# Four routing steps move to the odd iteration, and a normalisation moves behind the routing's places

## The reference

```python
h = tokens + pos_embed                                   # embedding
h = h + local_attn(layernorm(h), w_qkv, w_proj, b_proj)  # windowed attention
flat = layernorm(h).reshape(-1, 192)
probs = softmax(flat @ router_w.T)                       # 8 experts
top_w, top_i = top_k(probs, 2)
top_w = top_w / top_w.sum(-1)
for e in range(8):
    w_e = sum(top_w * (top_i == e), -1)
    out += w_e * (gelu(flat @ w1[e] + b1[e]) @ w2[e] + b2[e])
h = h + out
```

## Time and profile before

| | |
|---|---|
| median of 3 runs | 1567.22 us (1561.56 to 1568.72) |
| the profiled execution | 1561.32 us, of which the span 1559.5 us |
| TensorE matmul (PE) busy | 1429.6 us, 92% of the span |
| VectorE (DVE) busy | 1105.2 us, 71% |
| GpSimd (POOL) busy | 900.7 us, 58% |
| ScalarE (ACT) busy | 665.5 us, 43% |
| mean granted clock of TensorE | 0.973 of full |

### The profile page before, as it was taken

How to read it: one execution, slowest core, us unless ns; L and a number is a source line. 1 busy time by engine, 2 the same in 40 slices (tenths; PEclk the granted TensorE clock), 3 DMA queues, 4 the chain that set the end, 5 groups by cost and what they waited for, 6 DMA issues and landing times.

```text
span 1559.5 us, 51122 instructions
## 1 busy us (share of the span) xinstructions
PE 1429.6 (92%) x17688; PEld 1190.2 (76%) x17689; DVE 1105.2 (71%) x2824; ACT 665.5 (43%) x1150; POOL 900.7 (58%) x899
## 2 busy tenths in 40 slices
PE   4999998999999999999777789999999999999995
PEld 4788887888888888888555567777777777777774
DVE  2578887886877888788654776666666666666663
ACT  2455455454545455454435333333333333333331
POOL 4236566555656556565334875666666666666655
PEclk9999999998999999999878999999999999999998
DMA  5665665656565565655334375555554455555552
GB/s 173 182 183 151 196 169 151 187 162 174 162 198 159 154 192 158 186 165 159 76 64 78 72 150 81 76 75 74 73 75 72 74 78 74 75 73 74 75 72 31
DMA packets 305662, 189.18 MB, mean 121 GB/s; under 512 B 201977, under 2 KB 291397, under 8 KB 304477
## 3 DMA queue, kind: packets, MB, share of 16 engines
q1 hardware_dynamic: 241706, 118.06, 30.6%
q0 software_dynamic: 41680, 41.84, 17.8%
q10 hardware_dynamic: 22115, 27.08, 5.5%
HBM read 89.79 MB, written 65.29 MB: 99 GB/s over the span
## 4 chain that ended last, share of the span: by engine, by line
PE 53%; DVE 18%; POOL 9%; issue 9%; ACT 4%; ACTq 4%; DMA 2%; SPq 1%; DVEq 0%; POOLq 0%
PE qk L1086 7%; PE qk L1087 7%; PE qk L1088 7%; PE scores L1073 7%; PE near L1073 6%; ACTq L599 3%; POOL sorted_scratch L498 3%; PE far L1073 3%; PE token_bank L1073 3%; PE mixed L1073 3%; PE qk L1182 3%; DVE qk L978 3%; POOL payload L508 2%; DVE st L758 2%; PE near L1119 2%
## 5 line engine op out<-in xcount | busy, mean ns | idle before, releaser
L498 POOL DMA_INDIRECT sorted_scratch<-payload,place x212 | 223.6, 1055 | 57.8 <-issue 57.2
L1119 PE MATMUL near<-we,both_patches 128*120 128x192 f32 x1272 | 224.4, 334 | 19.2 <-DMA both_patches<-in_xt 11.6
L572 ACT ACTIVATE stage<-near,bias 128x384 f32<-128x384 f32 x118 | 68.5, 581 | 383.6 <-PE near L1073 368.0
L1119 PEld LDWEIGHTS near<-we,both_patches 128*120 128x120 f32 x1272 | 208.6, 186 | 29.7 <-issue 27.7
L483 POOL DMA_INDIRECT out<-both_patches,token x111 | 205.9, 1855 | 36.2 <-issue 36.0
L483 POOL DMA_INDIRECT out<-v_side,token x108 | 198.1, 1834 | 38.6 <-issue 37.9
L1086 PE MATMUL qk<-w_hi,stage 128*128 x666 | 165.5, 248 | 5.1 <-DVE v_side L911 5.1
L1086 PE MATMUL qk<-w_hi,both_patches 128*128 x648 | 160.2, 247 | 8.0 <-issue 4.1
L1088 PE MATMUL qk<-w_hi,we 128*128 x666 | 165.4, 248 | 0.0
L1087 PE MATMUL qk<-w_lo,stage 128*128 x666 | 165.4, 248 | 0.0
L1088 PE MATMUL qk<-w_hi,both_patches 128*128 x648 | 160.1, 247 | 0.0
(11 more groups left out here) (259 smaller groups left out, 3711.5 us busy)
## 6 DMA issues: line engine op xcount, KB each, us to landing
both_patches<-in_xt SPq DMA_DIRECT2D x53, 720.0 KB
v_diag<-v_scratch SPq DMA_DIRECT2D x159, 89.2 KB
v_scratch<-v_side SPq DMA_DIRECT2D x53, 191.2 KB, 3.7
tabs<-tab_scratch SPq DMA_DIRECT2D x53, 180.0 KB
out<-h ACTq DMA_DIRECT2D x52, 180.0 KB
stage<-in_w ACTq DMA_DIRECT2D x8, 1152.0 KB
k_diag<-qk SPq DMA_DIRECT2D x436, 15.8 KB
stage<-in_w ACTq DMA_DIRECT2D x8, 576.0 KB
```

Source lines behind the costliest of these rows:

```text
L498: pool.indirect_dma_start(out=sorted_dram, out_offset=bass.IndirectOffsetOnAxis(ap=at, axis=0), in_=payload[0:rows, 2 * (block % RING) + n ...
L572: act.activation(act_out[:, m, :], bank_of(u, m), ACT.Gelu, bias=bias[k % 2][:, m:m + 1], scale=1.0 / WS).then_inc(s["gelu_done"], 1)
L1119: ins = pe.matmul(near[0:ROWS, n * D:n * D + D], patches[f % 2][:, x, n * ROWS:n * ROWS + ROWS], we[:, x, :], start=(x == 0), stop=(x == K ...
```

## The change

The 26 steps are cut at two more points (`PART_AT`). The first four steps of the former part 1 (L802 to L805: the best expert masked, the second largest logit, where it is, times the ranks) become part 1 and run in the odd iteration right behind part 0; `choose(1)` and `marks` become part 2 and stay in the even one. The former part 3 is cut behind the places (part 4) and before the wait for the shares (part 5). In even iterations with routing due, `normalise` of the embedded block moves behind parts 3 and 4, ahead of part 5; in all others it moves behind the split of the expert weights (and behind the list of batches in iteration 51, and the splits of the attention weights in iteration 0). The step number that ScalarE's `second_share` waits for stays 7 in its group.

```diff
-PART_AT = (0, 5, 11, COUNTS_READ, STEPS)
+SECOND_AT = 7
+PART_AT = (0, 5, 9, 11, COUNTS_READ, 18, STEPS)
...
-                    act.wait_ge(s["step"], STEPS * grp + PART_AT[1] + 2)
+                    act.wait_ge(s["step"], STEPS * grp + SECOND_AT)
...
                     then(dve.tensor_tensor(tmp[:], tmp[:], ranks, ALU.mult))
+                if part == 2:
                     choose(1)
...
-                if part == 2:
+                if part == 3:
...
-                if part == 3:
+                if part == 4:
                     for j in range(CHOSEN):
...
-
+                if part == 5:
 
                     dve.wait_ge(s["weighed"], grp + 1)
...
                 if due:
-                    route_steps(grp, 1)
+                    route_steps(grp, 2)
...
-                if runs(t, 0):
-                    normalise(h1[f % H_RING], mv1, rs1, xn1, "1", f + 1)
                 if t == 0:
...
                 if due:
-                    route_steps(grp, 2)
                     route_steps(grp, 3)
+                    route_steps(grp, 4)
+                if runs(t, 0) and due:
+                    normalise(h1[f % H_RING], mv1, rs1, xn1, "1", f + 1)
+                if due:
+                    route_steps(grp, 5)
...
                     ins.then_inc(s["split_lo"], 1)
+                if runs(t, 0) and not due:
+                    normalise(h1[f % H_RING], mv1, rs1, xn1, "1", f + 1)
                 if due_0:
                     route_steps(grp_0, 0)
+                    route_steps(grp_0, 1)
```

## The result

The changed kernel takes 1586.68 us (median of 4 runs, 1583.38 to 1602.62), the one before 1567.26 in the same comparison: 1.0144 times as long (95% interval 1.0094 to 1.0194; it isn't the quotient of the two medians, 1.0124). The forecast was 1562.6, with a range of 1546 to 1577. The profiled execution after took 1583.38 us, 22 more than that of before; 19.8 of them lie in iterations 8 to 51. Lines of the file after stand 1 to 7 further down (L978 is L985, L812 is L814, L691 is L692).

A forecast was written before the change was run, and what follows sets the result against it. A ring through VectorE, ScalarE and TensorE was taken to bound the kernel. Pairs -12.7, +1.3 and +7.4, old low clocks -7.4, new ones +9.5, edges -2.7: together -4.6, from 1567.22 to 1562.6 us, range 1546 to 1577.

The forecast's parts named there:

- the count's wait: Even iteration: VectorE waits 0.8 us for TensorE's count before the places, where it waited 1.11 for GpSimd's `rs`.
- The odd cost: Odd iteration: four added steps and a meeting with GpSimd's L526 make L978 later by 0.9 to 1.4 us, taken 1.16.
- TensorE's 1.40: Odd iteration: TensorE's 1.40 us stand before its transposes, from a late exponential, would go.
- step 5 of the even iteration: VectorE's eight remaining steps end earlier, so L978 starts 2.6 us earlier, net 2.4, in ten even iterations.
- Three falls: Three of six even iterations where ScalarE issues an expert's weights fall to a low clock, 3.15 us each: +9.5.
- three old ones: Low clocks of odd iterations 19, 31 and 37 go: -7.4 us.
- The rival "slower": Clock falls in every weight iteration (8, 14, 20, 32, 38, 44), 5.2 us each: +17.1, 1584.3 us; chance 0.15.
- The full gain: Rival: odd iteration's added steps slip past L526, costing 0.89, and no new clock falls: -20.0, 1547.2 us; chance 0.25.
- Nothing: Rival: the `rs` wait and the moved steps are slack on VectorE, so no change: 1567.2 us; chance 0.12.
- the ring: Closed chain bounding iterations 8 to 51, 28.8 us a pair: VectorE's attention output, ScalarE's exponential, TensorE's logits, back to VectorE.
- The start: Iteration 0: the normalisation and its wait no longer stand ahead of L951, for which TensorE waits: 1.5 us less.

The follow-up runs named there:

- N: Against the kernel before, only the normalisation moved, in even and odd iterations; the four steps stay in the even one: 1548.35 us, ratio 0.9924.
- the extra steps: Four extra steps of the same shapes, on a scratch tile, added to N in the odd iteration: 1572.44 us, ratio 1.0126.

## Why the prediction was wrong, point by point

**Right: the parts that were read off one engine.** In iteration 24, L939 starts 0.80 after the exponential (forecast 308.43 - 307.62 = 0.81, before 2.47); the count's wait ends at 2.98 (3.18) and is 0.63 (0.8); L820 ends at 4.69 (4.68). L809 lasts 0.19. The odd cost from the logits to the low half is 2.52 - 1.53 = 0.99 in the mean (1.16, range 0.9 to 1.4). The trace agrees with the rule of the Trainium skill that the forecast weighed (SBUF — State Buffer, Who interferes with whom): L806 and L489 pay 0.79 and 0.91. TensorE's 1.40 ahead of the transposes is gone from iteration 23; in the odd iterations 14 stands of 0.2 to 2.6 became five of 0.3 to 0.7, and in the six weight iterations it stands 1.24 to 2.28.

**Wrong: step 5 of the even iteration, and with it the sum.** It said that L978 starts 2.6 earlier, net 2.4, in ten iterations, 0.9 in five, 0.1 in seven: 29.2 us, 1.33 a pair. Measured from the exponential to the attention output it is 11.50 - 11.01 = 0.49 against the first profile and 0.17 against the second. Over 22 pairs that is 10.8 us for the 29.2 forecast, and it makes most of the miss; the odd iteration cost 1.29 a pair, 28.4 us, for the 25.5 forecast (22 x 1.16). Three causes:
- The saving was counted as if VectorE alone decided when the low half starts. It waits for ScalarE's copy too. At 7.08 after the exponential the forecast was just past the earliest possible in the first profile (logits at 5.94 in iteration 22, plus 0.94). After the change the even logits come at 6.51 in the mean, and VectorE waits there 26 times in the whole span, 21 of them in the 22 even iterations from 8 to 50. Against the first profile, the low half starts 1.03 earlier after the exponential (8.61 to 7.58 in the mean). What left VectorE's queue became waiting: against N, the full change has the steps' work elsewhere and 26.7 us more idle time on VectorE (136.5 - 109.8). That leaving steps out gains nothing in N is shown; that late logits alone hold the even iteration of the full change is not, since no run could take them away.
- L991 (L984 before) was given 0.2 for a meeting with L527 that "may" come. In the even iterations it rose from 0.16 (no meeting in 22) to 0.76 (21 meetings), 0.60 each, and with it the link behind the low half from 2.89 to 3.43: half of the 1.03 is lost again. The meeting is not chance: a low half that waits for ScalarE's copy brings L991 to where L527 starts. In the odd iterations L991 fell from 0.62 to 0.39, as the meetings fell from 21 to 8.
- The odd link ahead of the logits rose from 5.37 to 5.99, which no term had. 0.44 of it is in the unchanged kernel's second profile as well.

**The two halves of the change.** By the times, N gains 0.0076, 12 us, and the four steps lose 0.0144 + 0.0076 = 0.022, some 34 us; the extra steps in the odd iteration alone lose 31.5. By the profiles, the extra steps make the odd iteration 0.72 longer than in N, the full change makes it 1.12 longer, and the even one 0.37. In the ordinary pairs (no weight iteration, no low clock in the pair or in the two iterations ahead: 11 pairs after, 13 in N) the full change is 1.14 a pair longer, 0.98 of it in the odd iteration. So the odd cost of 1.16 was about right, and the saving set against it in the even iteration, 0.89 and 0.77 for the four steps, was about nothing. Why the extra steps cost more by the times than by their profile stays open. One step of the odd sum doesn't follow from its rows: a fourth step that waits to L691 + 2.9 makes L978 1.56 late, not 1.25; the 1.16 is 1.56 less 0.40. That it is close to the mean is in part luck, as L806 met L527, on which it was built, in five of 22.

**The clock.** Three falls were priced at 9.5 and three old ones at -7.4; there were three after (iterations 14, 25 and 26) and four before, so about nothing in total. The rival "slower" had 1584.3 from six falls. The time is near it, but its mechanism is not what happened: of 8, 14, 20, 32, 38 and 44 only 14 fell. "The full gain" hung on added steps slipping past L527. In most odd iterations they did, and the gain stayed out all the same. "Nothing" put the ring in ScalarE and TensorE alone; for the even iteration's steps that holds, for the odd one it doesn't.

**Edges.** The start gave 0.7 of the 1.5 forecast, and behind iteration 51 the profile after is 2.9 us longer, of which no run shows the cause.

## What to carry to other kernels

Work moved off one iteration's queue is worth what is last there after the move, not its own length: before counting a saving, work out when every other operand of the next instruction arrives, and count an instruction where it lands at full price. An instruction that now waits for another engine's result starts in step with everything else that waits for it: look at what it runs beside (here 0.60 us in 21 of 22 iterations). Test a move by leaving the work out altogether: if that gains nothing, there is nothing to give in exchange for a new cost elsewhere. And profile the kernel before twice: its iterations 8 to 51 were the same to 0.01 us a pair while three of its eight links differed by 0.4 to 1.1.

## What the runs showed of the hardware

While GpSimd issued an indirect DMA and for some 2 us from its start, signals of TensorE to other engines came late against the modelled end of their matmuls, by 1.2 us in the median for the turns after the change and up to 2.4. That the matmuls themselves were not late is read from the distance of the signals: the ends of two turns are 0.34 apart by the records, and where both were late, most were signalled within 0.1 us of each other (20 of 27 after the change, 24 of 29 in the second profile of before). What behind the matmul was held, the records don't tell. Moving the scatter moved the delay from the turns (none late) to the scores (86 of 88). The 2 us are no sharp limit: with the scatter behind the scores, 14 turns due 2.22 us after the start of one were still 0.2 to 0.5 late. The Trainium skill says of SBUF's ports that TensorE and ScalarE never wait on anyone (SBUF — State Buffer, Who interferes with whom); the records of the matmuls agree, their signals here did not come on time. Why the first profile of the kernel before has the same scatters and no late signal stays open, and whether signals are late in executions without the profiler, no run shows.

A copy of VectorE can pay for a GpSimd instruction too: in iteration 24 L991 (128x24) took 0.91 instead of 0.17 beside L527, which began 0.05 earlier and took 0.93.
